# Four of the eight relation products of a graph layer by a seven-product scheme, with the root's product last

## What is computed

```python
u = x @ root + bias                       # x: (625, 1024), root: (1024, 1024)
for r in range(8):
    mask = (edge_type == r)
    sums = segment_sum(x[src] * mask[:, None], dst, 625)
    cnt = segment_sum(mask, dst, 625)
    u = u + (sums / maximum(cnt, 1)[:, None]) @ weight[r]
z = concatenate([u, x], axis=1) @ w_gate + b_gate
h = tanh(u) * z + x * (1.0 - z)
```

## Time and profile before

| | |
|---|---|
| median of 3 runs | 1142.08 us |
| lowest and highest | 1140.33 and 1142.98 us |
| span of the profiled execution | 1141.8 us |
| TensorE busy in it | 1096.1 us |
| VectorE busy | 665.4 us |
| ScalarE busy | 390.2 us |
| mean granted clock of TensorE | 0.978 of full speed |

### The profile page before, as it was taken

One profiled execution on the slowest core, in us unless ns is written; L12 is line 12 of the kernel. 1 busy time (PEld: TensorE's weight loads), 2 busy tenths in 40 slices (PEclk: granted clock), 3 DMA queues, 4 the chain that ended last, 5 costly groups with the idle time before them and its releaser, 6 DMA issues.

```text
span 1141.8 us, 14422 instructions
## 1 busy us (share of the span) xinstructions
PE 1096.1 (96%) x5505; PEld 915.6 (80%) x5505; DVE 665.4 (58%) x1408; ACT 390.2 (34%) x599; POOL 392.9 (34%) x272
## 2 busy tenths in 40 slices
PE   6989999999999999998999999799979999999996
PEld 5868888888888888888999999787756878878874
DVE  7585666666641122113766676466378738777647
ACT  3222223222222222223324323261433515347652
POOL 6044433688787887103232440000020000311016
PEclk9989999999999999999999999899989999989997
DMA  9968999999975556875999934442142011578757
GB/s 332 417 192 239 276 278 273 220 214 215 213 166 125 120 120 121 250 184 159 293 262 253 257 96 124 131 177 96 70 91 76 26 67 38 199 247 301 257 176 257
DMA packets 94467, 217.27 MB, mean 190 GB/s; under 512 B 29975, under 2 KB 46170, under 8 KB 85944
## 3 DMA queue, kind: packets, MB, share of 16 engines
q1 hardware_dynamic: 39482, 137.13, 36.3%
q0 software_dynamic: 37504, 48.18, 20.4%
q10 hardware_dynamic: 17406, 30.97, 10.1%
HBM read 149.53 MB, written 66.71 MB: 189 GB/s over the span
## 4 chain that ended last, share of the span: by engine, by line
PE 86%; DVE 8%; DMA 3%; ACT 2%; issue 1%; POOLq 0%; ACTq 0%; DVEq 0%; SPq 0%
PE ps L507 71%; PE ps L749 4%; PE ps L786 3%; DVE rl L353 2%; PE ps L713 2%; PE ps L497 1%; DVE EQ L1268 1%; DMA stage<-in_w_e 1%; PE ps L797 1%; PE ps L764 1%; DMA stage<-in_w_rel 1%; ACT rh L344 1%; PE ps L666 1%; PE ps L730 1%; DVE st L1217 1%
## 5 line engine op out<-in xcount | busy, mean ns | idle before, releaser
L353 DVE TENSOR_TENSOR rl<-stage,rh 128x512 fp32r<-128x512 f32 (+1 forms) x288 | 235.0, 834 | 356.7 <-ACT rh L344 339.5
L344 ACT CAST rh<-stage 128x512 fp32r<-128x512 f32 (+1 forms) x288 | 197.3, 707 | 511.2 <-PE ps L507 264.7
L507 PE MATMUL ps<-rh,xTh 128*125 128x512 f32 x800 | 317.1, 396 | 5.3 <-DVE U L1339 4.6
L1898 POOL DMA_INDIRECT adj_scratch<-cnt,idx x164 | 263.9, 1609 | 163.3 <-DVE EQ L1268 57.1
L507 PE MATMUL ps<-rl,xTh 128*125 128x512 f32 x800 | 315.5, 394 | 0.0
L507 PE MATMUL ps<-rh,xTl 128*125 128x512 f32 x800 | 315.2, 394 | 0.0
L507 PE MATMUL ps<-rh,Ar 125*125 125x342 f32 x600 | 191.5, 324 | 4.0 <-DVE rl L353 3.3
L507 PE MATMUL ps<-rl,Ar 125*125 125x342 f32 x600 | 190.8, 323 | 0.0
L507 PEld LDWEIGHTS ps<-rh,xTh 128*125 128x125 f32 x800 | 148.7, 186 | 43.3 <-DVE U L1339 5.0
L507 PEld LDWEIGHTS ps<-rh,xTl 128*125 128x125 f32 x800 | 149.0, 186 | 37.3
L507 PEld LDWEIGHTS ps<-rl,xTh 128*125 128x125 f32 x800 | 149.0, 186 | 36.3
(11 more groups left out here) (266 smaller groups left out, 1233.3 us busy)
## 6 DMA issues: line engine op xcount, KB each, us to landing
stage<-in_w_rel SPq DMA_DIRECT2D x32, 1024.0 KB
stage<-h_scratch SPq DMA_DIRECT2D x24, 855.0 KB
stage<-in_w_e SPq DMA_DIRECT2D x16, 1024.0 KB
adj_scratch<-Z POOLq DMA_DIRECT2D x16, 767.0 KB, 21.3
adj_scratch<-Z SPq DMA_DIRECT2D x16, 767.0 KB
h_scratch<-He ACTq DMA_DIRECT2D x40, 257.0 KB
h_scratch<-He ACTq DMA_DIRECT2D x40, 256.0 KB
KR<-key_scratch ACTq DMA_DIRECT2D x37, 256.0 KB
```

The costliest lines, as they stand in the source:

```text
L344: e.copy(h, s).then_inc(*a_hi.up(*[("hi", t) for t in step(i)]))
L353: e.tensor_tensor(l, s, h.bitcast(F32), ALU.subtract).then_inc(*v_lo.up(*[("lo", t) for t in step(i)]))
L507: ins = e.matmul(ps[0:P, b, 0:width], a, m, start=first and n == 0, stop=last and n == len(parts) - 1)
L1898: e.indirect_dma_start(accd[to], bass.IndirectOffsetOnAxis(ap=idx[:, n:n + 1], axis=0), cnt[:, n:n + 1], None, compute_op=ALU.add).then_in ...
```

## The change

The four last relations (units 5 to 8, `FAST`) are computed by Strassen's scheme. The inner dimension and the columns are cut in two, so the weights are four quarters b11, b12, b21, b22 of 512 x 512; the rows are two pairs of chunks (0 with 1, and 2 with 3) and the fifth chunk alone. Instead of eight quarter products of a pair there are seven, with sums of x quarters (four sums, S) on the left and sums of weight quarters (t1 to t4) on the right. The fifth chunk stays with eight tile products for each column half. In matmuls: a relation has 4 x (7 x 2 + 4) x 3 = 216 of 512 columns, where it had 240.

- **x sums.** S is made once, on VectorE (`s_made`, 20 subtractions and additions of 500 columns and 8 low parts) and ScalarE (`s_high`, 8 casts), in the third unit (`S_AT`), after its odd tiles.
- **Weight sums.** For each of the four relations VectorE makes t1 to t4 in `stage` places, eight additions of 1024 columns (`summed`). The relation then has 28 tiles to cast and subtract instead of 16.
- **Joining the products.** Partial sums leave PSUM and come back: ScalarE copies three (`V2`, `V5`), VectorE makes four (`V2`, `V3`) and seven further ones directly into `He`; the other three of the ten blocks of h are copied by ScalarE.
- **Places.** Three more staging places (`stageC`, `stageD`, `stageE`), and banks given by name (`where`) inside and after the four relations.
- **Order.** The relations come first and the root's product is the last (`UNITS`), so ScalarE reads out the first product and VectorE the last.
- **Windows.** The 41 key windows end in the fifth product (the first seven-product one) instead of the sixth. `WINDOWS` now has six or five windows in the halves of the second and of the fourth product, four in those of the third, and six in the fifth.
- **Waits.** GpSimd's first adjacency load and ScalarE's first adjacency cast also wait for the last seven-product relation. The bias load moves to before the root's product, and a load of spare x rows into unused partitions of `U` is added.

```diff
-WINDOWS = (0, 2, 4, 6)
+WINDOWS = {(0, 1): (0, 2, 4, 6), (1, 0): (0, 1, 2, 4, 5, 6), (1, 1): (0, 1, 3, 5, 6), (2, 0): (0, 2, 4, 6), (2, 1): (0, 2, 4, 6),
+           (3, 0): (0, 1, 2, 4, 5, 6), (3, 1): (0, 1, 3, 5, 6), (8, 0): (), (8, 1): ()}
+UNITS = [*range(1, R + 1), 0]
+FAST = (5, 6, 7, 8)
+KINDS = ("b11", "t2", "t3", "t1", "t4", "b21", "b22")
+KEYS_IN_FAST = (2, 7, 12, 17, 22, 26)
+S_AT = 2
...
+            def fast_unit(u, of):
...
+                for j in range(4):
+                    for p in range(2):
+                        ends(part("b11", j, ("W", p), x_stat(j, 2 * p), j == 0, j == 3), "b11", j, ("W", p), ("E", 1))
+                    ends(part("b11", j, ("E", 1), x_stat(j, 4), j == 0, j == 3), "b11", j, ("E", 1), ("E", 1))
+                for j in range(4):
+                    for p in range(2):
+                        ends(part("t2", j, ("X", p), s_stat(1, p, j), j == 0, j == 3, ("s lo", 1, p)), "t2", j, ("X", p), ("X", 1))
+                banks.drop(("fast", u, "X", 0), ("fast", u, "X", 1))
...
+                held["Z", 1] = banks.take(("fast", u, "Z", 1), ("he", u, 2, 1), where=held["X", 0][0])
+                held["E", 2] = banks.take(("fast", u, "E", 2), ("he", u, 4, 1), where=held["X", 1][0])
...
             def adjacency_copy(r):
                 on.wait_ge(*at("acb", r))
                 if r == 0:
                     on.wait_ge(*at("slot zero"))
+                    on.wait_ge(*at("fast", FAST[-1], "b22", ("E", 2)))
...
+            for n, unit in enumerate(UNITS):
+                if unit in FAST:
+                    for l in range(FL):
+                        highs(F0[unit] + l + RT)
+                        if l in KEYS_IN_FAST:
+                            g = next_key_rows(g)
+                    continue
                 for hf in range(2):
-                    if unit or hf:
+                    if n or hf:
                         for k in range(8):
                             highs(unit_tile(unit, hf, k) + RT)
...
+                            if k in WINDOWS[n, hf]:
+                                g = next_key_rows(g)
+                            if n == S_AT and k % 2:
+                                s_high((4 * hf + k // 2) % 4, hf)
...
+            def fast_before(i):
+                for u in FAST:
+                    if i - F0[u] == 17:
+                        for p in range(2):
+                            on.wait_ge(*at("fast", u, "t2", ("X", p)))
+                            on.wait_ge(*at("v1", u, p))
+                            e.tensor_tensor(V2[0:P, p, :], ps[0:P, banks.of["fast", u, "X", p], :], V2[0:P, p, :], ALU.add).then_inc(*v_out.up(("v2", u, p)))
...
+            def fast_after(i):
+                for u in FAST:
+                    of = fast_loads[u]
+                    if i - F0[u] == 1:
+                        summed(u, "t1", 0, 0, 1, 0, ("loaded", of["b12"]), *split_off(u, "b11", 0))
+                    if i - F0[u] == 3:
+                        summed(u, "t1", 1, 0, 1, 0, ("loaded", of["b12"]), *split_off(u, "b11", 1))
+                        for h in range(2):
+                            summed(u, "t2", h, 0, 2, 3, ("loaded", of["b22"]), ("made", u, "t1", h), *(split_off(u - 1, "t4", h) if u != FAST[0] else ()))
+                    if i - F0[u] == 5:
+                        summed(u, "t3", 0, 1, 2, 1, ("made", u, "t1", 0))
+                        summed(u, "t4", 0, 3, 4, 3, ("loaded", of["b21"]), *split_off(u, "t2", 0))
...
+            def s_made(n, p):
...
             for r in range(2):
                 on.wait_ge(*at("added", NG - 2))
                 on.wait_ge(*at("added", NG - 1))
+                for c in (0, 2, 4):
+                    on.wait_ge(*at("he", FAST[-1], c, 1))
```

407 lines of the change are left out of this document (328 added, 79 removed).

## The result

The changed kernel takes 1157.66 us (median of four runs, 1156.25 to 1158.71), the kernel before 1142.53 us beside it (1140.33 to 1146.18): a ratio of 1.0127, 95% interval 1.0103 to 1.0152. It is slower by 15 us, and the forecast was 1157. The profiled execution has a span of 1155.8 us, 14.0 us more than before.

A forecast was written before the change was run, and what follows sets the result against it. TensorE's x W matmuls bound the kernel before; after the change ScalarE and VectorE in turns would set the pace in the early halves. 1141.8 - 22.2 + 32.3 + 9.9 - 4.8 = 1157 us, range 1145 to 1168 (0.65).

The forecast's parts named there:

- The bound: x W stage: TensorE's matmuls set the pace, so 96 fewer take 22.2 us off if TensorE is fed.
- place 4: First seven-product relation: the fourth product waits for VectorE's V2 read, 19.6 us after ScalarE's first copy; 10 us late.
- Turns and halves: Halves a and b of products 1 to 3, counted from 0: ScalarE and VectorE in turns make TensorE 32 us late.
- The block of x sums: Halves 2a and 2b: vector operations and casts in turns add 13.9 us each, bounds 8 and 17.
- The start: Half 0b: the stall up to 79.54 us taken as unchanged, bounds -2 and +3 us.
- The three other relations: Seven-product relations after the first: TensorE stays fed, nothing lost; bounds 0 and 4.8 us each.
- Rival 3: Seven-product relations not fed: strict turns and a late weight quarter, 54.7 us for each of three; 1171 us, chance 0.07.
- The end: End of the x W stage: no copies there and the adjacency cast earlier; 4.8 us off, bounds 0 and 5.
- Rival 1: Halves 1a to 3b and place 4: looser turns, TensorE keeps the pace; 1115 us; chance with its half-case 0.13.
- Rival 2: Five halves where TensorE falls idle: slow clock of 2.75 us each adds 14 us; 1171 us, chance 0.08.
- Rival 4: Nothing to be seen: x sums and place 4 at low bounds, start 2 us better; about 1142 us, chance 0.07.
- The signs listed: If right: stops of 5 us or more in 1a, 2a, 2b, 3a; casts waiting over 142.5 us; stage end near 543.

The follow-up runs named there:

- later_loads: The changed kernel with ScalarE's key load started for the window three further on instead of four, so it waits one window less: 1153.91 us, ratio 1.0097.
- windows4: The changed kernel with four key windows in each half again up to the fourth product, six in each of the first two seven-product relations: 1154.67 us, ratio 1.0087.
- before_later_loads: The kernel before with only the key loads waiting one window less: 1137.91 us, ratio 0.9949.
- zero_at_once: zero_sooner, but the second scratch matrix zeroed beside loads 6 to 9, four pieces each, and `SOLE` = 4: 1119.49 us, ratio 0.9787.
- two_scratches_early: The changed kernel with `SOLE` 8 instead of 10: GpSimd adds into both scratch matrices from the 9th group of edges: 1157.22 us, ratio 1.0113.
- before_windows: The kernel before with only the key windows moved as in the changed kernel, no sums or seven-product relations: 1149.55 us, ratio 1.0043.
- later_and_early: later_loads with `SOLE` = 8, so GpSimd adds in pairs from the 9th group: 1135.54 us, ratio 0.9964.
- zero_sooner: later_and_early with fewer windows near the x sums, the second scratch zeroed two loads sooner and `SOLE` = 6: 1115.51 us, ratio 0.9795.

## Why the prediction was right, and where its steps were off

**The bound.** That a matmul taken away is worth its full time "as long as nothing else sets the pace" was the sentence on which all hung, and something else did. Forecast were 42.2 us of lateness (32.3 and 9.9) against 22.2 us off; 43.1 came, counted as the forecast counts, from the first stop on (33.8 and 9.3, see place 4). later_loads shows the cause as given: with the key load out of the window's way, six stops of 29.5 us in all become three of 7.5, the one for V2 is gone too, the stage ends 38.6 us sooner, and nothing else was changed.

**Turns and halves.** Each term of the sum of the halves is right to 0.8 us or better, 1.5 us in all. The block of x sums (13.9 us, between bounds of 8 and 17) came out at 14.2 and 14.7: operations and casts do go in turns there. The formula of the Trainium skill ("VectorE: DVE Perf Modes", TRN2 errata) gives an estimate of 678 ns for such an operation, which would add 1.4 us over both halves. Measured were 1.1 us more (0.3 and 0.8); that is too little to tell it from the other links of a block.

**The start.** "I take it unchanged; bounds -2 and +3" is the term of the sum that was furthest off. The first stop lies 3.4 us later (82.94 against 79.54), outside those bounds. The root's product had been read out by VectorE; now ScalarE makes five copies, one behind another, and its next casts stand behind them. The rows of ScalarE in the kernel before, and of ScalarE and SyncE in the kernel after:

```profile
37.03 1.06 ACT L967 CAST xTh<-ps 128x500 fp32r<-128x500 f32 x2 [5.22 <-PE ps L497]
```

```profile
38.35 1.06 ACT L1166 CAST xTh<-ps 128x500 fp32r<-128x500 f32 x2 [5.22 <-PE ps L572]
...
46.48 0.59 ACT L1105 COPY He<-ps 125x512 f32<-125x512 f32 x1 [1.54 <-PE ps L582]
47.46 3.22 ACT L404 CAST rh<-stage 128x512 fp32r<-128x512 f32 x6 [0.40 <-ACT He L1105]
...
49.51 2.74 SPq L468 DMA_DIRECT2D stage<-in_w_rel  x2
```

The weight load that waits for those casts goes out at 49.51 instead of 47.91, 1.6 us later. I had said that the load waits for the same low part. That is so, but the low part waits for a cast, and the cast for the copies. Yet the copies are the small part of it. ScalarE is 1.3 us late already at 38.35, ahead of the first copy, and that is no effect of the order: this cast starts between 37.03 and 38.88 us in the profiled executions of either order. From this cast to the weight load it is 11.15 or 11.16 us in the nine kernels with the root's product last and 10.87 or 10.88 in the four with it first: 0.3 us for the copies. The larger part is the load's flight, 11.99 instead of 9.27 us in the chain. That one does go with the order: from the load's start to the first cast that waited for it are 11.4 to 12.4 us in the nine and 9.1 to 9.5 in the four. The three parts are 4.3 us; 0.9 is made good before the stop, where it is 21.4 instead of 22.3 us from that cast to TensorE's start. So some 2 us of the 3.4 are the change's, inside the bounds, and the rest was there by chance: windows4, where that cast of x starts at 37.11, has its first stop at 81.32, 1.8 us later than before. That the longer flight is due to the five stores of h was not tried.

**Place 4.** From the first copy (291.23) to V2's read and its end is 19.6 us, as worked out:

```profile
291.23 0.58 ACT L1105 COPY He<-ps 125x512 f32<-125x512 f32 x1
...
310.13 1.29 DVE L1439 TENSOR_TENSOR V<-ps,V 125x512 f32<-125x512 f32 x2
```

The wait was 4.99 instead of 7.2 us, because TensorE came later: behind the stop at 291.95 nine matmuls ran 0.43 us apart (1.8 us). What the pair costs in all from there follows from the stage's end: 24.3 + 22.2 - 3.4 - 33.8 (the halves, 1.5 more than 32.3) = 9.3 us, forecast 9.9.

**The three other relations.** No stop in them, as taken. Rival 3 (strict turns, 54.7 us each) fell: here the ten tiles of lead are enough.

**The end.** 4.8 us were forecast and 7.4 gained. Of the other 2.6, 2.0 is a shorter wait of TensorE for VectorE between the relations' sums and the gate. Its length goes with the number of seven-product relations (5.0 to 5.5 us with none or two, 3.1 to 3.5 with four), and why is open. The errors of the sum cancel, which is luck: +3.4 at the start, +1.5 in the halves, -0.6 in place 4, -2.6 at the end and -2.9 behind it make -1.2, and 1157 becomes 1155.8. What the matmuls take off and what the pair adds came out as worked out, without luck; the 1.2 us are luck.

**Rival 1** (pair fast enough, 1115) was wrong for this change: the turns of one tile take 4.45 us, far above its 3.4. With the turns undone and the adjacency in time the kernel reaches 1115.51, with gains in it that the rival did not have (before_later_loads alone has 6 us). **Rival 2** fell by 14 us: the granted clock is 0.50 from 80 to 85 us and 0.66 from 115 to 120, yet the distances of the stops are those of the pair, and the slow clock is missing from the stops themselves: 32.9 - 27.7 - 2.75 = 2.45 for 1a (measured 2.21), 38.2 - 27.7 - 2.75 = 7.75 for 2b (7.55), 33.1 - 27.7 - 2.75 = 2.65 for 3a (2.71). Only behind the stop for V2, where TensorE sets the pace afterwards, does the slow clock count, and there the forecast had it. The rule of the Trainium skill ("TensorE: Matmul & The Clock Gate", HAM oscillation), that an engine which goes idle each round pays for the fall each round, agrees with the trace in the fall itself, which comes again at nearly each stop; in this trace it adds nothing to the time where another engine sets the round. The windows of the kernel after, with granted clock third from the right:

```profile
80.00:85.00 5.00, 2.06 (x5) 1.67 (x6) 2.34 (x7) 2.28 (x4) 3.96 (x3) 0.50 0.91 310
115.00:120.00 5.00, 4.18 (x11) 3.19 (x12) 0.69 (x1) 3.12 (x6) 3.08 (x2) 0.66 1.02 336
```

**Rival 4** (nothing to see) fell too: it needed the x sums and place 4 at their low bounds and an earlier start, and none came.

**The signs listed.** Stops of 5 us or more were named for 1a, 2a, 2b and 3a. Only 2a (8.76) and 2b (7.55) have them; 1a and 3a have 2.21 and 2.71, because the slow clock of the stop before takes 2.75 us of the room. The numbers stood in the prediction and were not subtracted; the sum did not need them. "Casts waiting for VectorE more than 142.5 us" came out at 138.1 for the windows alone, and 13.8 more for the weight sums, so it came only with both; 142.5 was the figure of the windows alone, and the sign should have named both. The stage ends at 548.06, where "near 543" was named: 3.4 us of the difference are the start and 0.9 the halves and place 4. The others came: granted clock under 1 between 100 and 300 us, no idle in places 5 to 7, no 3.28 us wait.

## What to carry to other kernels

An engine that is not the bound has a schedule of its own: before matmuls are taken away, add up the round of the engines that feed them, with every wait that stands in their streams, and see how much of it fits. A DMA start that waits for the instruction its own neighbour has just begun makes two engines take turns. Made to wait for the window before, the same load brought ScalarE's waits for windows down from 138.1 to 39.4 us, but it had less time to land, and once other transfers crowded it (zero_at_once) that showed. And a stage made shorter shows the next one in line: an edit that alone was worth nothing (`SOLE`) was worth 15 us once the first bound was gone, so test such edits together, and look whether an edit that changes nothing did what it was meant to (two_scratches_early).

## What was not expected of the hardware

- **A stop and the slow clock are not tied by the stop's length alone.** After stops of 0.52, 0.73 and 1.91 us (before_windows) and 1.60 (before_later_loads) the first matmul took 0.49 to 0.50 us, and where it was looked at (before_windows, 110 to 115 and 225 to 230 us) the granted clock stayed 1.00. After 2.71 us and more it was mostly 0.79 at once, and after 2.21 us 0.62. But after 1.57 us (after, 291.95), 2.24 (later_loads, 163.40, granted clock 0.69 from 165 to 170) and 3.79 (zero_at_once, 107.15, 0.81 from 110 to 115) the first matmul took 0.47 to 0.50 us, and only some matmuls later the distance rose to 0.43. So the first matmul behind a stop does not tell its price; the distances of the next dozen do.
- **Additions in two scratch matrices.** The counts of the same 41 groups were in for a first adjacency load at 494.69 (later_loads), 479.88 (later_and_early), 467.26 (zero_sooner) and 453.13 us (zero_at_once) with `SOLE` at 10, 8, 6 and 4: 13 to 15 us for each two groups, though the windows and the zeros differ between some of them. It is no rule: with `SOLE` at 8 alone (two_scratches_early) the zeros came too late for it and the load went out at 504.51, and the two kernels with the old order and `SOLE` at 10 differ by 15 us (461.33 in the kernel before, 476.41 in before_later_loads).
- **Zeros closer together hold up other loads.** With four pieces beside a load instead of two, the key loads between 75 and 110 us took 17.4 us to land instead of 7.3, and stops of 3.79 and 1.55 us came back. `SOLE` was changed in the same run, and which of the two crowds the key loads was not tried apart.
